# A two-layer graph kernel whose row tiles are turned by DMA and VectorE instead of by TensorE

## What is computed

```python
h = max(layernorm(x), 0)
for l in range(2):
    m_left, m_right = h @ W_left[l].T, h @ W_right[l].T
    u_left  = h @ m_left.T  / sqrt(768)          # per graph, 64 x 64
    u_right = h @ m_right.T / sqrt(768)
    u = u_left * triu(adj) + u_right * swap(triu(adj, 1))
    e = exp(u) * adj
    h_lin = h @ W_lin[l].T + b_lin[l]
    ctx = (e / (sum(e, 2) + 1e-10)) @ h_lin
    h = relu((ctx - mean) / (std + 1e-3) * ln_a[l] + ln_b[l])
out = x + h
```

## Time and profile before

| | |
|---|---|
| median of 3 runs | 2858.11 us (2855.97 to 2859.23) |
| span of the profiled execution | 2857.3 us |
| PE busy | 2820.9 us (99%), 15880 matmuls |
| DVE busy | 1546.2 us (54%) |
| ACT busy | 691.1 us (24%) |
| DMA queue of SP and ACT | 125984 packets, 153.91 MB, 17.6% of 16 engines |
| mean granted TensorE clock | 0.996 |

### The profile page before, as it was taken

How to read it: one execution, slowest core, us unless ns; L and a number is a source line. 1 busy time by engine, 2 the same in 40 slices (tenths; PEclk the granted TensorE clock), 3 DMA queues, 4 the chain that set the end, 5 groups by cost and what they waited for, 6 DMA issues and landing times.

```text
span 2857.3 us, 43013 instructions
## 1 busy us (share of the span) xinstructions
PE 2820.9 (99%) x15880; PEld 2577.6 (90%) x15880; DVE 1546.2 (54%) x3426; ACT 691.1 (24%) x1271; POOL 109.6 (4%) x209
## 2 busy tenths in 40 slices
PE   7999999999999999999999999999999999999997
PEld 6999899998899988999989999899998899998996
DVE  5555565555555555655555555455545555554556
ACT  3322222322223222232332222112221122221121
POOL 0000000000000000000000000000000000000000
PEclk9999999999999999999999999999999999999998
DMA  5111011110111111111241121121211111111211
GB/s 160 40 41 42 34 51 40 46 44 26 49 40 46 44 40 35 46 46 52 62 127 57 55 61 61 55 72 50 61 61 53 63 54 56 61 61 55 72 34 57
DMA packets 127178, 157.63 MB, mean 55 GB/s; under 512 B 65440, under 2 KB 83872, under 8 KB 127136
## 3 DMA queue, kind: packets, MB, share of 16 engines
q1 hardware_dynamic: 125984, 153.91, 17.6%
q10 hardware_dynamic: 1152, 3.15, 0.4%
HBM read 100.40 MB, written 52.43 MB: 53 GB/s over the span
## 4 chain that ended last, share of the span: by engine, by line
PE 98%; DVE 1%; DMA 1%; SPq 0%; ACT 0%; issue 0%; DVEq 0%; ACTq 0%
PE pm L546 55%; PE pm L609 28%; PE pu L597 6%; PE pc L633 5%; PE pc L537 3%; DMA rows<-in_x_dram 0%; DMA side<-in_L_gnn_W_lin_dram 0%; PE pu L620 0%; SPq L389 0%; SPq L378 0%; DVE side L789 0%; DVE rows L852 0%; DVE side L852 0%; DVE rows L842 0%; DVE side L842 0%
## 5 line engine op out<-in xcount | busy, mean ns | idle before, releaser
L546 PE MATMUL pm<-ht,wt 128*128 128x256 f32 (+1 forms) x8064 | 1636.5, 360 | 1.3 <-DVE ht L722 1.3
L546 PEld LDWEIGHTS pm<-ht,wt 128*128 128x128 f32 x8064 | 1352.7, 189 | 215.6 <-issue 1.7
L609 PE MATMUL pm<-wt,ht 128*128 128x384 f32 x4608 | 845.4, 337 | 0.6 <-DVE hl L722 0.6
L609 PEld LDWEIGHTS pm<-wt,ht 128*128 128x128 f32 x4608 | 794.0, 188 | 6.8 <-DVE hl L722 6.8
L722 DVE TENSOR_TENSOR gt<-pm,gt 128x512 fp32r<-128x512 f32 x384 | 265.4, 691 | 814.4 <-ACT gt L678 814.4
L678 ACT CAST gt<-pm 128x512 fp32r<-128x512 f32 x384 | 224.0, 583 | 1197.6 <-PE pm L546 1197.6
L722 DVE TENSOR_TENSOR hl<-pm,hl 128x384 fp32r<-128x384 f32 x256 | 142.5, 557 | 390.6 <-ACT hl L683 389.6
L683 ACT CAST hl<-pm 128x384 fp32r<-128x384 f32 x256 | 123.0, 480 | 551.1 <-PE pm L609 551.1
L597 PEld LDWEIGHTS pu<-gt,ht 128*128 128x128 f32 x1536 | 211.6, 196 | 9.7
L597 PE MATMUL pu<-gt,ht 128*128 128x256 f32 x1536 | 214.7, 282 | 0.0
L633 PE MATMUL pc<-hl,et 128*128 128x386 f32 (+1 forms) x768 | 158.7, 342 | 3.1 <-DVE et L722 1.8
(11 more groups left out here) (60 smaller groups left out, 848.5 us busy)
## 6 DMA issues: line engine op xcount, KB each, us to landing
rows<-in_x_dram SPq DMA_DIRECT2D x64, 384.0 KB, 3.2
h_dram<-side SPq DMA_DIRECT2D x64, 384.0 KB, 2.3
rows<-h_dram SPq DMA_DIRECT2D x64, 384.0 KB, 3.2
side<-in_x_dram SPq DMA_DIRECT2D x64, 384.0 KB, 3.3
out_dram<-side SPq DMA_DIRECT2D x62, 384.0 KB, 2.6
mask<-in_adj_dram SPq DMA_DIRECT2D x48, 128.0 KB, 3.6
side<-in_L_gnn_W_left_dram SPq DMA_DIRECT2D x12, 384.0 KB, 3.7
side<-in_L_gnn_W_right_dram SPq DMA_DIRECT2D x12, 384.0 KB, 3.6
```

Of the source, the lines that this page charges most:

```text
L546: last = nc.tensor.matmul(pm[:, k % M_BANKS, t0 * P:t1 * P], wt[:, lr, a, kc, oc * P:(oc + 1) * P], ht[:, kc, t0:t1, b, :], start=(kc == 0 ...
L609: last = nc.tensor.matmul(pm[:, j % M_BANKS, 0:HALF], ht[:, kc, t, a, :], wt[:, LIN, b, kc, half * HALF:(half + 1) * HALF], start=(n == 0) ...
```

## The change

TensorE no longer transposes anything. A row tile is read from DRAM in pieces of 32 numbers (128 bytes), so placed that each 32x32 square lies where it belongs after the turn but is itself unturned; one VectorE transpose of 128x768, which works in 32x32 squares, puts it into the new buffer `turned`, from which ACT and DVE split it into `ht` (steps TX and T). Such a load is four DMAs with 768 pieces each. In layer 0 the normalised x is written to a new DRAM buffer h0 first and read back from there. The W blocks and, in layer 0, the adjacency go the same way (eight DMAs of 128 pieces for a group's adjacency instead of one). X and N are spread over the M-phase; side 1 is done in one piece. One buffer `turned` serves all tiles. Weight loads are all issued by SP.

```diff
-    steps = [("H", 0, 0), *v[0], ("H", 0, 1), ("S", 5), ("U", 0), ("U", 1), ("H", 1, 0), ("EX",), ("EM",), ("EP",),
-             ("T", 0), ("H", 1, 1), ("adj",), *v[1], ("H", 2, 0), ("T", 1), *v[2], ("ET",),
-             *[("X", 3, 1)] * norm_next, ("H", 2, 1), ("C", 0), *v[3]]
-    steps += [("H", 3, 0), ("T", 2)] + ([("N", 3, 1)] if norm_next else []) + [*v[4], ("H", 3, 1), *v[5], ("T", 3)]
-    extra = {(0, 1): [("C", 1)], (1, 1): [("A",), ("F", 0)], (3, 1): [("C", 2)], (4, 1): [("F", 1)],
-             (6, 1): [("C", 3)], (7, 1): [("F", 2)], (8, 1): [("F", 3)]}
+    steps = [("H", 0, 0), *v[0], ("H", 0, 1), ("S", 5), ("U", 0), ("U", 1), ("TX", 0), ("H", 1, 0), ("EX",), ("EM",),
+             ("EP",), ("T", 0), ("H", 1, 1), ("adj",), *v[1], ("TX", 1), ("H", 2, 0), ("T", 1), *v[2], ("ET",),
+             ("TX", 2), ("H", 2, 1), ("C", 0), *v[3], ("H", 3, 0), ("T", 2), ("TX", 3), *v[4], *v[5], ("T", 3),
+             ("H", 3, 1), ("C", 1)]
+    extra = {1: [("A",), ("F", 0)], 3: [("C", 2)], 4: [("F", 1)], 6: [("C", 3)], 7: [("F", 2)], 8: [("F", 3)]}
...
+    if norm is not None:
+        for t, at in enumerate((2, 5, 8, 10)):
+            after.setdefault(at, []).append(("X", t, norm))
+            after.setdefault(at + 1, []).append(("N", t, norm))
...
+    for k in range(K_SIDES):
+        if k == 0:
+            steps += [("M", k, 0, 2), ("M", k, 2, 4)]
+        else:
+            steps += [("M", k, 0, 4)]
...
+    start = [("X", 0, 1), ("X", 1, 1), ("N", 0, 1), ("X", 2, 1), ("N", 1, 1), ("X", 3, 1), ("N", 2, 1), sides[0],
+             ("N", 3, 1), ("TX", 0), ("T", 0), ("TX", 1), sides[1], ("T", 1), ("TX", 2), ("T", 2), ("TX", 3), ("T", 3),
+             sides[2]]
...
+            def load_turned(dst, source, loaded):
+
+                quads = source.rearrange("(q b) (c p a) -> p b c q a", q=Q, p=Q, a=32)
+                for p in range(Q):
+                    sp.dma_start(dst[32 * p:32 * p + 32, :].rearrange("b (c q a) -> b c q a", c=KC, q=Q),
+                                 quads[p]).then_inc(loaded, 16)
...
+                    if kind == "N":
+                        t = step[1]
+                        X = G + step[2]
+                        sp.wait_ge(x_norm, tile_count(X, t + 1))
+                        sp.dma_start(tile_rows(h0, X, t), row_slot(X, t)).then_inc(n_stored[row_sem(X, t)], 16)
+                        if first + step[2] == 0:
+                            if t >= 2:
+                                sp.wait_ge(n_stored[t - 2], 16)
+                                load_h(h0, 0, t - 2)
...
+                            sp.wait_ge(n_stored[(t + 1) % 2], 32 * X + 16 * ((t + 1) // 2) - 16)
+                            if t < 3:
+                                load_rows(X, t + 1)
+                            if t >= 2:
+
+                                sp.wait_ge(h_turned, tile_count(X, t - 3))
+                                load_h(h0, X, t - 2)
+                    if kind == "TX":
+                        t = step[1]
...
+                        if t < 2 or not norms and first + 2 < GROUPS:
+                            sp.wait_ge(h_turned, tile_count(N, t + 1))
+                        if t < 2:
+                            if first + 1 < PER:
+                                load_h(h0, N, t + 2)
...
+                    if kind == "T":
+                        t = step[1]
+                        act.wait_ge(h_turned, tile_count(N, t + 1))
+                        if first >= 0:
+                            act.wait_ge(m_full, M_JOBS * G + H_JOB + 2 * t + 2)
...
+                        nc.scalar.copy(ht_tile(t, HI), by_graph(turned[:])).then_inc(ht_hi, 1)
...
+                    if kind == "TX":
+                        t = step[1]
+                        dve.wait_ge(h_loaded[t % 2], h_count(N, t))
+                        wait_from(dve, ht_split, tile_count(N, t))
+                        nc.vector.transpose(turned[:], rows[:, t % 2, :]).then_inc(h_turned, 1)
+                    elif kind == "T":
+                        t = step[1]
+                        dve.wait_ge(ht_hi, tile_count(N, t + 1))
+                        low_part(ht_tile(t, LO), by_graph(turned[:]), ht_tile(t, HI)).then_inc(ht_split, 1)
...
+                        nc.vector.transpose(mask[:, :, ADJ, :], adj_in[:]).then_inc(mask_ready, 1)
```

More of the change, by code:

```diff
@@ L132, in regions @@
+    extra = {k: [sides[k + 3]] for k in range(9)}
+    extra[1] = extra[1] + [("A",)]
+    for j in range(6):
+        extra[3 + j] = extra[3 + j] + [lins[j]]
+    parts = [(-1, 0, False, start + m_phase_steps(extra, 2))]
     half = groups // 2
-    steady0 = iteration_steps(True, True, True)
+    steady0 = iteration_steps(True, True)
     parts.append((0, 1, False, steady0))
     parts.append((1, half - 2, True, steady0))
-    parts.append((half - 2, half - 1, False, iteration_steps(True, True, False)))
@@ L145, in regions @@
[L145 to L150, removed]
+    parts.append((half - 2, half - 1, False, iteration_steps(True, False)))
+    mixed = [sides[7], lins[0], sides[8], lins[1], sides[9], lins[2], sides[10], lins[3], sides[11], *lins[4:]]
+    late = {k: [step] for k, step in enumerate(mixed)}
+    change = iteration_steps(True, False, sides[:6], late)
@@ L329, in kind_count @@
-        def kind_count(G, step):
[L331 to L343, removed]
+            return 2 * (N - PER) + 3 * PER + 2 if layer else 3 * N + 3
@@ new lines, in h_count, with w_index, w_stage, w_count @@
+        def h_count(N, t):
+            return 32 * TURNS * N + 16 * TURNS * (t // 2 + 1)
+        def w_index(G, step):
+            return WEIGHT_STEPS.index(step, 0 if G < 0 else W_JOBS)
+        def w_stage(i):
+            if i >= W_JOBS:
+                return STAGES + i % 2, side[:, 2 + i % 2, :]
+            return i % STAGES, side[:, i % STAGES, :] if i % STAGES < 2 else vec[:, 0, :]
+        def w_count(i):
+            first = 0 if i < W_JOBS else W_JOBS
+            on = STAGES if i < W_JOBS else 2
+            at = range(first + (i - first) % on, i + 1, on)
+            return 16 * sum(TURNS if WEIGHT_STEPS[j][0] == "W" else 1 for j in at)
@@ L344, in next_block @@
+        def kind_count(G, step):
+            return sum(s[0] == step[0] for s in WEIGHT_STEPS[:w_index(G, step) + 1])
+        def next_block(i):
+            on = STAGES if i < W_JOBS else 2
             return i + on if i % W_JOBS + on < W_JOBS else None
@@ L432, in walk @@
+                    if first == PER - 2 and step == ("TX", 0):
+                        for i in range(2):
+                            sp.wait_ge(n_stored[i], row_count(PER - 1, 2 + i))
+                            load_weights(W_JOBS + i)
                     if kind == "adj":
                         sp.wait_ge(e_masked, G + 1)
-                        if not layer:
-                            sp.wait_ge(adj_t_stored, 16 * G + 16)
                         if first == PER - 1:
+                            sp.wait_ge(adj_t_stored, 16 * PER)
@@ L466, in walk @@
                             load_vectors(1)
-                    if first == PER - 2 and step == ("N", 3, 1):
-                        for i in range(W_JOBS, W_JOBS + 2):
-                            load_weights(sp, i)
+                if first < 0:
+                    sp.wait_ge(n_stored[2], 16)
+                    sp.wait_ge(n_stored[3], 16)
+                    load_vectors(0)
                 if first == PER - 1:
@@ L551, in walk @@
             def walk(part, G):
-                first, end, looped, steps, _, _ = part
+                first, end, looped, steps = part
                 N = G + 1
@@ L614, in walk @@
                         last.then_inc(m_full, 1)
-                    elif kind == "A" and next_layer == 0:
-                        pe.wait_ge(adj_loaded, 32 * N + 32)
-                        wait_from(pe, u_joined, pair_count(N, 0, 2))
-                        for t in range(TILES):
-                            both = mask[:, t, ADJ:MR + 1, :].rearrange("p a b -> p (a b)")
-                            last = nc.tensor.transpose(pu[:, t, 0:P], both, ident[:])
-                        last.then_inc(a_full, 1)
                     elif kind == "C":
@@ L636, in walk @@
                 if fresh:
-                    pe.wait_ge(c_clear, ring_after(part, G, [s for s in steps if s[0] == "W"][-1]) + C_BANKS)
+                    pe.wait_ge(w_split, KC if first < 0 else 2 * KC)
             each_part(pe, walk)
```

375 lines of the change are left out of this document (174 added, 201 removed).

## The result

The median is 2852.3 us against 2856.7 us for the kernel before on the same chips (16 runs each); the ratio, taken from undisturbed runs alone, is 0.9985, 95% interval 0.9978 to 0.9992. The change is worth 0.15%, where 1.4% was forecast. By the forecast's own bound (0.2%) that is "no difference", to which it gave 0.06. The profiled execution has a span of 2851.4 us.

A forecast was written before the change was run, and what follows sets the result against it. TensorE, busy 99% of the span, was taken to bound the kernel: 2857.3 - 98 spared + 43 H(2,0) + 6 C 0 + 7 prologue + 2 group 15 gave 2817 to 2818 us span, 2819 median; range 2780 to 2900.

The forecast's parts named there:

- What TensorE is spared: TensorE's transposes and side 1 in one piece: 3.26 us a group in layer 0, 2.82 in layer 1; 98 us in all.
- The wait before H(2,0): H-phase: TX 0 delays VectorE's split of H(1,0), so TensorE stalls 1.4 us a group, 43 us in all.
- The wait before C(0): End of H-phase, where TensorE needs `et`: stall of 0 to 0.3 us, taken as 0.2 a group, 6 us in all.
- three paths to `et`: Before C 0: TensorE's arrival at 14.0 us, VectorE's order about 14.0, SP's issues and `ebd` data at 11.0 + T.
- the time T of a load in the DMA engines: How long a small-piece tile load keeps its engines busy: 2.3 to 2.6 us, upper bound 9, taken as 2.6.
- The prologue: Start of kernel: normalised rows go to DRAM and back, second half of side 0 at about 33 us; +7 us (2 to 14).
- about 13 us: Prologue: when SP starts the first store of normalised rows, after its initial 16 DMAs are out.
- Group 15 and the one behind it: Group 15 loses six W blocks, 6.7 us; its 3 us wait becomes another of about that length, +2 (-3 to 8).
- small pieces clog the queue: Rival at C 0: from T = 4.5 us, 23 ns a piece, the stall eats the gain left; 2999 at upper bound; chance 0.17.
- rival 3: A wait in each group makes TensorE's clock drop, 1.7 us lost in each of 31 groups, 2872 us; chance 0.08.
- covered, barely: Tile 3's load lands near 19 to 20 us after S 5, TX 3 is due about 20.6, so no wait.
- The remark that pieces of 256 bytes land as fast as those of 512: DMA loads: the rows don't show the skill's penalty for pieces under 512 bytes; if it held, the slower rival would apply.

The follow-up runs named there:

- places experiment: Kernel after, steps unchanged; on SP's queue the prologue's adjacency moved behind four tile loads, group 14's weight blocks behind EP, vectors to group 15's end: 2841.3 us, ratio 0.9947.
- the ends: Kernel after with EP, then H(1,0), ahead of TX 0, adjacency behind TX 1, prologue adjacency behind all tile loads, vectors at group 15's end: 2813.7 us, ratio 0.9853.

## Why the prediction was wrong

- What TensorE is spared was right. In layer 1 a group without any wait would take 87.37 - 2.82 = 84.55 us; with the waits of the kernel after, 1.45 and 0.7, that is 86.7, and 86.75 was measured.
- The wait before H(2,0), 1.4 us from the order of VectorE's queue, was right in place, size and cause (1.44 us in the timeline). So was the transpose, 0.974 us on average against 0.95.
- The wait before C(0) was the step that failed: 0.7 us for 0.2. The step weighed three paths to `et` and put SP's issue at 0.45 us a DMA, near the 0.42 us of an adjacency DMA, for DMAs of a shape that the trace before did not show. They take 0.59 us, and in a loop SP adds about 0.14 us of register work to each: 2.92 us for four instead of 1.8. The bounds were put on another unknown, the time T of a load in the DMA engines, and that was well sized. At the queue's measured shares the bytes of a tile take 1.3 us of each of 16 engines (24.8% of 2829 us for 207.43 MB) and 192 pieces at 6 ns 1.2 us more, 2.5 us as an estimate, for the 2.6 of the forecast. An `ebd` DMA landed 2.4 us after its issue (median), 2.2 when it was ahead of the load and 2.1 before. The cost sat in front of the engines. 31 groups x 0.5 us: 15 of the 33 us that are missing.
- Group 14 (5 us) was missed outright: the text of the change has two weight loads at TX 0, ahead of EP, and the forecast followed SP's queue only in the steady groups. With the two blocks moved behind EP the wait of 3.5 us before C(0) is gone and group 14 takes 88.15 us for 91.4, which shows the cause; 1.6 of the 5 us were the clock behind that wait.
- The prologue was to cost 7 us and cost 12. The step "about 13 us" for the first store was right (12.28 us); too small was the issue time again. Tile 2 was asked for at 24.05 us instead of 22, because the load of tile 1 kept SP until 23.25, and the second half of side 0 started at 36.1 us instead of 33. Behind it TensorE waited 1.6 and 2.4 us for VectorE, where two to three were put. The adjacency's nine DMAs ahead of the first store are within the 13 us: moving them gave 2.8 us in the places experiment and 3.8 in "the ends".
- Group 15 and the one behind it were to be 4.3 us shorter together and were 2.3 us longer. The wait for the last W block was 5.2 us, behind the vectors (1.6 and 1.0 us in the two runs with them moved). A wait of 3.2 us for tile 3 before side 0 was not foreseen: the split of tile 3 stands behind a V step, and for its weight block ScalarE waited 3.4 us. Behind these two waits the clock took 3.7 us.
- Of the rivals, none came true as a whole. The one by which small pieces clog the queue has a 23 ns threshold that the measured cost does not come near, though its sign, C(0) waiting for `et` and that for the `ebd` DMA, did appear, by the issue. The clock kept 1.00 behind the 1.4 us of the steady groups (0.994 in the mean), as the forecast argued, but a price near rival 3's 1.7 us a group was paid in groups 14, 15 and 16: 5.3 us. The Trainium skill, "DMA: Bandwidth & Descriptors", Specifications, says that pieces under 512 bytes are read, modified and written. Here that shows at most as those 6 ns a piece; the cost that ruled was not in the transfer.
- That tile 3's load was "covered, barely" was right for TensorE, though the turn of tile 3 starts only 21.8 us after S 5, 0.46 us late, where the load was put at 19 to 20. It mattered more than it seemed: it made layer 0 get slower when EP was put right alone.
- The median lies inside the range of 2780 to 2900 us by luck: the range was kept wide for the rivals, not for SP's issue time or the groups 14 to 16, where the loss came from.
- The remark that pieces of 256 bytes land as fast as those of 512 compares 128 KB with 384 KB, so it said nothing of what a small piece costs.

So the gain was eaten by where the turning stands in the queues more than by its amount. 98 us were saved. 45 went to the wait before H(2,0), some 30 of them to the transpose (0.97 us a group) and the rest to U, which T 0 had covered. Some 22 went to `et` behind SP's issues (31 x 0.7), 12 to the prologue and 12 more to groups 14 to 16, 5 of these by the clock. With nothing but the order changed, 41 us of that come back.

## What to carry to other kernels

When a saturated engine is relieved, list for each queue the steps that it was just in time for, and put new work behind those, not ahead of them: here 1 us of VectorE ahead of a split cost TensorE 1 us, thirty-one times. Price a DMA on its issuing queue as well as in the engines, with the number of DMAs, and follow that queue also through the one group that differs. Two waits in series on in-order queues may have one cause, and undoing one can uncover a third: change the order of a neighbour together with it, and read each layer's groups apart. A single wait of several us can cost TensorE more than its length: look at the granted clock behind it.

## What the runs showed of the hardware

A VectorE transpose of 128x768 fp32 takes 0.974 us, about what a two-input operation of the same width takes (0.957), and one of 128x256 takes 0.43. One of 128x32 takes 0.206. Splitting the same bytes into pieces of 128 bytes instead of 3072 costs the DMA engines 6 ns a piece, but makes the issue of such a DMA on SP's queue last 0.59 instead of 0.32 us, and 0.57 with pieces of 64 bytes; a block with the same number of pieces in rows of six was issued in 0.38 in the kernel before and in 0.54 in the kernel after. A wait of 1.4 us on TensorE in each group did not bring its granted clock down in the steady groups. Behind a wait of 5.2 us it was granted 0.50 for the next 3.2 us. Waits of 1.7 to 2.9 us were followed by the lower clock in some groups of a kernel and not in others.
